# First norm of a macaron block: expert-in-rows logits, weights asked for between the chunks, first turned chunk not stored

## The reference, cut to what matters

```
x = x + 0.5 * ffn(layernorm(x))          # first half, where the change is
x = x + attention(layernorm(x))
x = x + 0.5 * ffn(layernorm(x))

def ffn(x):
    shared = (silu(x @ shared_w1) * (x @ shared_w2)) @ shared_w3     # 256 -> 1024 -> 256
    scores = sigmoid(x @ router_w)                                   # 16 experts
    top 2 of (scores + expert_bias) per token; gate = their scores
    routed = sum over experts of swiglu(x; w1, w2, w3 of expert) * gate   # 256 -> 256 -> 256
    return shared + routed
```

## Time and profile before

| | |
|---|---|
| median of 3 runs | 1538.68 us (1537.26 to 1539.66) |
| the profiled execution | 1533.96 us, span 1532.1 us |
| PE busy | 1453.8 us, 95% of the span |
| DVE, ACT, POOL busy | 963.5, 663.0, 587.5 us |
| first slice of 40 (38.3 us), PE busy | 4 tenths |
| `norm_first` | from 0 to about 64 us |

### The profile page before, as it was taken

One profiled execution on the slowest core, in us unless ns is written; L12 is line 12 of the kernel. 1 busy time (PEld: TensorE's weight loads), 2 busy tenths in 40 slices (PEclk: granted clock), 3 DMA queues, 4 the chain that ended last, 5 costly groups with the idle time before them and its releaser, 6 DMA issues. The chain is left out here.

```text
span 1532.1 us, 29046 instructions
## 1 busy us (share of the span) xinstructions
PE 1453.8 (95%) x8999; PEld 1186.4 (77%) x9032; DVE 963.5 (63%) x2019; ACT 663.0 (43%) x1339; POOL 587.5 (38%) x832
## 2 busy tenths in 40 slices
PE   4999999999989987999999999979999999999998
PEld 4888888888878775667666666648888888888887
DVE  4578865555545575776776676535776455555566
ACT  2334444343333443656655665553222344433332
POOL 5608850133333005453554464231188333333100
PEclk9999999999999998999999999979999999999999
DMA  9696899635375855445555544536464634356941
GB/s 321 244 362 226 312 348 361 234 104 185 104 248 198 287 185 132 95 107 140 133 129 136 131 123 108 155 114 222 173 243 157 213 108 145 104 175 225 298 135 55
DMA packets 176804, 286.32 MB, mean 187 GB/s; under 512 B 20754, under 2 KB 125714, under 8 KB 176418
## 3 DMA queue, kind: packets, MB, share of 16 engines
q1 hardware_dynamic: 134914, 206.83, 42.9%
q0 software_dynamic: 19104, 56.64, 10.2%
q10 hardware_dynamic: 22656, 21.11, 4.7%
HBM read 144.20 MB, written 110.36 MB: 166 GB/s over the span
## 5 line engine op out<-in xcount | busy, mean ns | idle before, releaser
L1574 PE MATMUL f_bank<-f_xparts,f_sw 128*128 128x512 f32 x1536 | 377.3, 395 | 4.0 <-DVEq L1505 3.1
L1574 PEld LDWEIGHTS f_bank<-f_xparts,f_sw 128*128 128x128 f32 x1536 | 284.1, 191 | 59.3 <-DVEq L1505 3.3
L1068 POOL DMA_INDIRECT outputs_by_choice<-f_yr,f_home x160 | 153.4, 959 | 366.7 <-DVE f_yr L1529 302.7
L2273 DVE TENSOR_REDUCE at_mx<-at_ps 128x1 f32<-128x384 f32 (+3 forms) x352 | 213.8, 632 | 111.0 <-PE at_ps L2402 104.5
L2167 ACT ACTIVATE at_pT<-at_ps 128x512 f32<-128x512 f32 (+1 forms) x352 | 194.3, 559 | 71.6 <-PE at_ps L2418 62.7
L2083 POOL TENSOR_SCALAR_AFFINE_SELECT at_pT<-at_pT 128x128 f32<-128x128 f32 (+2 forms) x352 | 124.0, 361 | 219.8 <-ACT at_pT L2167 215.5
L1026 POOL DMA_INDIRECT rows_by_slot<-f_xq,slot x128 | 147.6, 1153 | 125.7 <-DVEq L1267 87.4
L2418 PE MATMUL at_ps<-fa_qT,fa_kT 98*128 98x256 f32 (+3 forms) x512 | 171.1, 386 | 5.7 <-DMA fa_qT<-at_mT 3.4
L1518 DVE TENSOR_TENSOR f_sil<-f_sil,f_bank 128x256 f32<-128x256 f32 x160 | 67.4, 421 | 170.2 <-ACT f_sil L1171 168.3
L1422 DVE TENSOR_TENSOR f_hid<-f_sil,f_bank 128x512 f32<-128x512 f32 x128 | 87.8, 686 | 125.7 <-PE f_bank L1574 123.7
L1151 ACT CAST f_hparts<-f_hid 128x512 fp32r<-128x512 f32 x128 | 79.3, 620 | 201.1 <-DVE f_hid L1422 201.1
(11 more groups left out here) (247 smaller groups left out, 2496.1 us busy)
## 6 DMA issues: line engine op xcount, KB each, us to landing
f_ring<-weights_in_parts SPq DMA_DIRECT2D x32, 768.0 KB, 5.6
weights_in_parts<-fa_whi SPq DMA_DIRECT2D x30, 768.0 KB, 8.4
f_rawx<-rows_by_slot ACTq DMA_DIRECT2D x152, 128.0 KB, 2.1
at_whi<-weights_in_parts SPq DMA_DIRECT2D x16, 768.0 KB, 8.0
fa_ew<-in_L_ffn_routed_w_dram SPq DMA_DIRECT2D x42, 256.0 KB, 5.5
rows_by_slot<-zero POOLq DMA_DIRECT2D x10, 1024.0 KB, 21.3
f_xq<-xn_rows POOLq DMA_DIRECT2D x32, 256.0 KB, 5.4
fa_ew<-outputs_by_choice SPq DMA_DIRECT2D x8, 1024.0 KB, 9.5
```

The lines of the kernel that those rows point to most:

```text
L1068: nc.gpsimd.indirect_dma_start(dram.yk, bass.IndirectOffsetOnAxis(ap=home[:, i:i + 1], axis=0), yr[:, i % 4, :], None).then_inc(y_st[i % 4 ...
L1574: ins = pe.matmul(ps[j % 2][:, :], sw12[:, wp, k, w, j * P:(j + 1) * P], xparts[:, u, xp, k, :], start=(i == 0), stop=(i == 3 * KD - 1))
L2273: v.tensor_reduce(own, ps1[i % RING1][:, 0:heads * w].rearrange("p (j a x) -> p j a x", a=min(heads, 2), x=w), AX.X, ALU.max).then_inc(mx_ ...
```

## The change

- The logits of a chunk are computed with the router's 16 columns as the stationary matrix and the whole turned chunk (512 tokens) as the moving one, into `psE` with the experts in partitions. ACT copies them to SBUF (`logit_rows`, into `turned_l`), and PE turns them, four small transposes a chunk (`turn_logits`), into `psL`. DVE's copy of the logits comes one chunk later than before.
- SP asks for weight pieces 3, 4, 5 and the attention weights between the chunks' stores; only pieces 0, 1 and 2 are still asked for ahead of them. The loop over chunks is written out. Attention's first weight work on ACT comes one chunk later, and so does DVE's.
- The turned chunk 0 is not stored. The waits for stores of the even buffer count 16 less.
- The end of the block doesn't wait for the stores of the attention weights any more. SP waits for them ahead of the load of expert 3, and DVE ahead of `places()`.
- DVE's normalize waits for PE's turn of chunk c-2 by itself (`turned`).

```diff
@@ norm_first
+        psE = m.ps("psE", [P, 2, CHUNK])
+        turned_l = m.sb("turned_l", [z.E, 2, CHUNK])
+        routed = m.sem("routed")
+        l_in = m.sem("l_in")
...
-            def store(c, c2, u, more):
+            def store(c):
+                u = c % 2
                 sp.wait_ge(normed, c + 1)
                 sp.sem_inc(g.held, 1)
-                sp.dma_start(dram.xn[bass.ds(c * CHUNK, CHUNK), :].rearrange("(t p) d -> p t d", p=P), xn[:, u]
+                sp.dma_start(dram.xn[c * CHUNK:(c + 1) * CHUNK, :].rearrange("(t p) d -> p t d", p=P), xn[:, u]
                              ).then_inc(xn_out[u], 16)
-                if more:
-                    sp.wait_ge(x_in[u], c2 * 16 + 32)
+                if c + 4 < z.NC:
+                    sp.wait_ge(x_in[u], 16 * (c // 2) + 32)
                     sp.sem_inc(g.held, 1)
                     load(c + 4, u)
-                sp.wait_ge(xnT_in, c + 1)
-                sp.sem_inc(g.held, 1)
-                sp.dma_start(dram.xnT[:, :, bass.ds(c * CHUNK, CHUNK)], xnT[:, u]).then_inc(xn_out[u], 16)
+                if c > 0:
+
+                    sp.wait_ge(xnT_in, c + 1)
+                    sp.sem_inc(g.held, 1)
+                    sp.dma_start(dram.xnT[:, :, c * CHUNK:(c + 1) * CHUNK], xnT[:, u]).then_inc(xn_out[u], 16)
...
-            for i in range(3, 6):
-                load_piece(i)
-            for i, w in enumerate((dram.W_q, dram.W_k, dram.W_v)):
-                sp.dma_start(att.wraw[:, :, i], w.rearrange("(k p) n -> p k n", p=P)).then_inc(a_in, 16)
-            with sp.Fori(0, z.NC // 2 - 2) as c2:
-                for u in range(2):
-                    store(c2 * 2 + u, c2, u, True)
-            for c in range(z.NC - 4, z.NC):
-                store(c, c // 2, c % 2, False)
+            for c in range(z.NC):
+                store(c)
+                if c == 0:
+                    load_piece(3)
+                elif c == 1:
+                    load_attention(0)
+                    load_attention(1)
+                elif c == 2:
+                    load_attention(2)
+                    load_piece(4)
+                elif c == 3:
+                    load_piece(5)
             sp.wait_ge(a_lo, 8 * KD + 1)
...
             for u in range(2):
-                sp.wait_ge(xn_out[u], 32 * (z.NC // 2))
+                sp.wait_ge(xn_out[u], 32 * (z.NC // 2) - 16 * (1 - u))
             sp.wait_ge(bias_in, 16)
-            sp.wait_ge(a_out, 32)
@@ DVE
             def normalize(c, c2, u, first):
                 dve.wait_ge(rs, c + 1)
                 if not first:
-                    dve.wait_ge(xn_out[u], c2 * 32)
+                    dve.wait_ge(xn_out[u], c2 * 32 - 16 * (1 - u))
+                    dve.wait_ge(turned, c - 1)
...
-                if not first:
-                    logits(c - 2)
+                if c >= 3:
+                    logits(c - 3)
...
-                if c >= 4:
-                    low_weights(c - 4)
+                if c >= 5:
+                    low_weights(c - 5)
             normalize(z.NC - 1, z.NC // 2 - 1, 1, False)
+            logits(z.NC - 4)
+            low_weights(2)
             low_weights(3)
@@ PE
-            def route(c, u, first):
+            def route(c, u):
                 pe.wait_ge(xnT_in, c + 1)
-                if not first:
+                if c >= 2:
+                    pe.wait_ge(l_in, c - 1)
+                for k in range(z.KD):
+                    ins = pe.matmul(psE[0:z.E, u, :], g.rw[:, k, :], xnT[:, u, k, :], start=(k == 0), stop=(k == z.KD - 1))
+                ins.then_inc(routed, 1)
+
+            def turn_logits(c, u):
+                pe.wait_ge(l_in, c + 1)
+                if c >= 1:
                     pe.wait_ge(logit_in, c)
                 for t in range(CT):
-                    for k in range(z.KD):
-                        ins = pe.matmul(psL[:, t * z.E:(t + 1) * z.E], xnT[:, u, k, t * P:(t + 1) * P],
-                                        g.rw[:, k, :], start=(k == 0), stop=(k == z.KD - 1))
+                    ins = pe.transpose(psL[:, t * z.E:(t + 1) * z.E], turned_l[:, u, t * P:(t + 1) * P],
+                                       g.ident[0:z.E, 0:z.E])
                 ins.then_inc(logit, 1)
...
+            for c in range(2, z.NC):
+                turn(c, c % 2, False)
+                route(c - 1, 1 - c % 2)
+                turn_logits(c - 2, c % 2)
+            route(z.NC - 1, 1)
+            turn_logits(z.NC - 2, 0)
+            turn_logits(z.NC - 1, 1)
@@ ACT
                 if not first:
-                    act.wait_ge(xn_out[u], c2 * 32)
-                    act.wait_ge(logit, c - 1)
+                    act.wait_ge(xn_out[u], c2 * 32 - 16 * (1 - u))
+                    act.wait_ge(routed, c - 1)
...
+            def logit_rows(c):
+                act.wait_ge(routed, c + 1)
+                if c >= 2:
+                    act.wait_ge(logit, c - 1)
+                nc.scalar.copy(turned_l[:, c % 2, :], psE[0:z.E, c % 2, :]).then_inc(l_in, 1)
...
             for c in range(2, z.NC):
                 chunk(c, c // 2, c % 2, False)
                 if c < 7:
                     high_piece(c - 1)
-                if c == 2:
+                logit_rows(c - 1)
+                if c == 3:
                     act.wait_ge(a_in, 48)
...
+            logit_rows(z.NC - 1)
@@ feed_forward, SP
                 for e in range(4):
+                    if e == 3:
+
+                        sp.wait_ge(pre.a_out, 32)
                     load_expert(e)
@@ feed_forward, DVE
                         if n == INVERT_AT:
+                            if not exact:
+                                dve.wait_ge(pre.a_out, 32)
                             places()
```

More of the change, by code:

```diff
@@ L122, in norm_first @@
         a_lo = m.sem("a_lo")
-        a_out = m.sem("a_out")
+        a_out = pre.a_out = m.sem("a_out")
         KD, E = z.KD, z.E
@@ L161, in _, with load_attention @@
                 load_piece(1 + u)
-            for i in range(3, 6):
-                load_piece(i)
-            for i, w in enumerate((dram.W_q, dram.W_k, dram.W_v)):
-                sp.dma_start(att.wraw[:, :, i], w.rearrange("(k p) n -> p k n", p=P)).then_inc(a_in, 16)
-            with sp.Fori(0, z.NC // 2 - 2) as c2:
-                for u in range(2):
-                    store(c2 * 2 + u, c2, u, True)
-            for c in range(z.NC - 4, z.NC):
-                store(c, c // 2, c % 2, False)
+            def load_attention(i):
+                sp.dma_start(att.wraw[:, :, i], (dram.W_q, dram.W_k, dram.W_v)[i].rearrange("(k p) n -> p k n", p=P)
+                             ).then_inc(a_in, 16)
+            for c in range(z.NC):
[10 more added lines that the diff above has]
+                    load_piece(5)
             sp.wait_ge(a_lo, 8 * KD + 1)
@@ L319, in _ @@
             pe.wait_ge(rw_in, 16)
-            route(0, 0, True)
-            with pe.Fori(1, z.NC // 2) as c2:
-                for u in range(2):
-                    turn(c2 * 2 + u, u, False)
-                    route(c2 * 2 + u - 1, 1 - u, False)
-            route(z.NC - 1, 1, False)
+            route(0, 0)
+            for c in range(2, z.NC):
[5 more added lines that the diff above has]
+            turn_logits(z.NC - 1, 1)
         @block.scalar
@@ L345, in _ @@
             high_piece(0)
+            logit_rows(0)
             act.wait_ge(x_lo, 1)
@@ L354, in _ @@
                     act.wait_ge(a_scaled, 1)
-                elif c < 7:
-                    k, half = (c - 3) // 2, (c - 3) % 2
+                elif c >= 4:
+                    k, half = (c - 4) // 2, (c - 4) % 2
                     for i in range(2):
                         nc.scalar.copy(columns(att, 0, k, i, half), given(att, k, i, half)).then_inc(a_hi, 1)
-                    if c == 6:
+                    if c == 7:
                         nc.scalar.copy(att.wv[:, 0], att.wraw[:, :, 2]).then_inc(a_hi, 1)
+            logit_rows(z.NC - 1)
 def pieces(z, raw12, raw3, to):
```

## The result

The changed kernel takes 1522.81 us (median of 4 runs, 1521.6 to 1524.12), the kernel before 1538.72. The ratio is 0.990, 95% interval 0.9878 to 0.9922, so 12 to 19 us faster. A later comparison gave 1524.54 against 1537.54, ratio 0.9918 (0.9896 to 0.9939). What both intervals hold is 12 to 16 us. The forecast was 7.8 us and 1530.9, with a range that ended at 1526.0: the direction was right, the size was half.

The account below looks back on a forecast made before the run. PE was taken to bound the kernel, so an earlier feed_forward start shortens it: 8.5 us from the first block less 0.7 given back makes 7.8, from 1538.7 to 1530.9 us. Range: 1526.0 to 1535.0.

Parts of the forecast that it names:

- Part 1: First block: new DMA order and unstored turned chunk 0 end normalize(7) at 45.3 us instead of 52.1, winning 6.8 us.
- Part 2: First block: three or four normalizes meet POOL's low parts; only that at chunk 7 costs, ending 47.5 instead of 45.3.
- Part 3: Logits on PE: products 1.8 us, transposes 0.8 us; PE's work per chunk falls from over 5.0 to 4.5 us.
- Part 4: First block's tail after normalize(7): 9.0 us instead of 11.7, winning 2.7 us.
- Part 5: Start of feed_forward: attention weights still queued delay turned chunk 2, ACT waits 0 to 4 us; 0.7 us given back.
- (e): Rival: thinner PE work in the first block lowers PE's clock into feed_forward, making the kernel slower; chance 0.02.
- no waits beyond the bytes: Rival, first block: stores land without the added 0.5 MB, no collision; gain 12 us or more, 1526 us; chance 0.04.

Follow-up runs that it names:

- second profile: The changed kernel, unchanged, profiled again on another chip: start of feed_forward at 53.56 us, ratio 0.9918; the kernel before, also profiled again: start at 65.13 us, ratio 0.9988.

## Why the prediction was wrong, point by point

**Part 1, the queue: right, with one hit by luck.** Normalizes 2 to 7 were forecast to start at 16.5, 23.6, 29.2, 36, 40 and 44 to 45 us, and started at 16.20, 22.78, 28.55, 34.47, 40.16 and 45.00. Chunk 6 is the lucky one: the turned store of chunk 4, for which it had to wait, had landed at 38.47, and what the normalize waited for was DVE itself, late from the held normalize of chunk 5. Most of this gain is the order; the store that is left out is 2.2 to 3.4 us of it, by the run that has it back, a meeting at chunk 7 included.

**Part 2, meetings of DVE and POOL: right in kind.** Two normalizes were held, by 2.0 us each (three in the second profile), but not that of chunk 7, so its end came at 46.37, between my 45.3 and 47.5. With POOL made to stand behind, the start is 2.1 to 3.2 us earlier, so the meetings cost 2 to 3 us, on the path; I had those ahead of chunk 7 at nothing. The exclusive lock of which the Trainium skill speaks (SBUF — State Buffer, "SBUF: two separate sides") is what the 3.41 beside POOL's 2.34 looks like. The Trainium skill gives it there for certain forms of DVE's instructions only (a two-port mode, or two inputs from SBUF); whether the normalize is one of them no run here shows.

**Part 3, the logits: the products right, the comparison wrong.** The 1.7 to 1.9 us for two products were measured as 1.89, and as 3.60 at the low clock. The transposes took 0.4, where I took 0.8. The step of the prediction that failed is this comparison. It took the old 3.43 us, and the turn's 1.95, for durations at full clock, because the clock column of before reads 1.00 in the first block, and set them against new products priced from a row at full clock. In the trace of before itself stood what speaks against it: 1.95 us for eight transposes, and 8.36 us for 24 products that take 2 x 2.91 later. The first block of before ran at the low clock throughout: its eight turns take 1.94 to 1.97 us, and the trace's record of the clock begins with a rise at 70.59 us. The old logits take 1.86 at full clock, so at full clock the new list is no shorter on PE. What the new form brought is the higher clock, and the end of the chain of copies in the tail, 4.1 us of it by the run with two banks.

**Part 4, the tail: mis-sized.** Forecast 9.0 from the end of normalize(7) to the last copy; it was 53.70 + 0.23 - 46.37 = 7.6. The block's end came at 53.9, where I had taken 55.5 (64.0 - 8.5). The tail's steps ran at full clock, and their transposes were cheap: a turn of 1.09 for 1.95, and twice 0.4 for 0.8, make up 1.7 us. The gain in the tail, 2.7 in the forecast, was 12.9 - 8.3 = 4.6 up to the start. Without the moved wait 3.8 to 5.0 of the whole would be lost, as part 4 said.

**Part 5, given back: wrong, there was nothing.** ACT was idle for 1.29 us ahead of turned chunk 2 (0.21 in the second profile), 48.0 and 48.2 us behind the start, where I had 48.8 to 51. But PE's pace across it is unchanged: its groups of 12 products start at 100.97 and 105.47, 4.5 us apart, as at that step before. The wait fitted in slack.

**Left out: the start at full clock.** The first 24 products of feed_forward take 5.70 us in the first profile, against 8.36: 2.7 us that no term of the sum had. In the second profile it is 7.32 against 7.49. So this term is 0.2 to 2.7 (of which 2.2 are left at the ranks); what decides whether the clock falls there was not settled.

**The sum.** For the profiles: start 10.3 to 11.6 us earlier (8.5 taken); first products 0.2 to 2.7 (none taken); nothing given back (0.7 taken). That makes 12 to 13 us, against 7.8: 1.8 to 3.1 us more from the start, 0.2 to 2.7 from the first products, and 0.7 not given back; the measured 12 to 16 agree with it in their lower half. What lies above is not assigned to a part of the change, and the two pairs of profiles have it behind the first block, where profiles of any kernel differ by up to 9 us. The rival of a clock that falls (e) was the wrong way round: before, it was low already, and the change brought it up. The range's end was set by "no waits beyond the bytes", which kept the old durations for the turns and put the first products at nothing.

## What to carry to other kernels

Before costing PE work, check one duration that is known at full clock (a 128 x 128 transpose, a 512-column product) inside the stretch in question, whatever the clock column says; if it is doubled, price old and new work at both levels. Then look at what ends last: six idle products a chunk brought a turn from 1.97 to 1.04 us, and the start stayed where it was (63.04 against 62.73, 55.18 against 54.70). DMAs that a ring of two buffers waits for belong in the queue ahead of weights needed later, and a simple count of bytes in order forecast four such waits to within 1.9 us in both profiles. At the end of a block, look at what stands between two short steps of another engine: a second PSUM bank and one copy moved were worth 4.1 us, where the new form brought 8.0 to 9.2. And try the parts of a change apart and together: here they are worth 2.7 and 1.3 us apart, and 10.8 to 11.9 together.

## What was not expected of the hardware

- The granted clock's column read 1.00 in the whole first block of before, while PE's work there took the time of the low level (turn 1.95, against 1.04 to 1.09 at full clock; the same in both profiles of before). It first reads 0.50 in the changed kernels after a fall that can be seen. The trace says why: its record of the clock begins at 70.59 us (68.97 in the second), with a rise to full inside the first 24 products, and the column prints 1.00 where there is no record. In the changed kernel the record begins at 19.72 us, just where the turns go from 1.97 to 1.24 and 1.09.
- The old logits never brought the clock up in the first block, though PE was busy for 5.00 of 5 us from 35 to 40 us. Their weight loads filled it (PEld 5.00), and the moving side had 16 columns. In the runs with 512-column products there, whether new logits or idle ones, it rose. Which of the two properties matters no run tells apart.
- A f32 product shows as two records in the trace and an f32 transpose as one; with 512 columns a product takes 0.95 us at full clock and 1.8 at half.
- The same 24 products at the start of `feed_forward` took from 5.70 to 8.36 us over the sixteen profiles, and 5.70 to 7.98 behind the same gap of 1.04 us. So a gain or a loss of under 3 us there can be the clock alone.
